# Delta-rule recurrence on one core: next step's products before this step's caps

## What is computed

```
def _cap(S):
    n = jnp.sqrt(jnp.sum(S * S, axis=(-2, -1), keepdims=True))
    return S / jnp.maximum(1.0, n / float(DK))

def step(carry, x):
    S_f, S_s = carry
    qt, kt, vt, bt, fdt, sdt, fgt, sgt = x
    S_f = fdt * S_f
    S_s = sdt * S_s
    err_f = vt - k_t . S_f
    err_s = vt - k_t . S_s
    S_f = S_f + b_t k_t err_f
    S_s = S_s + b_t k_t err_s
    S_fc = _cap(S_f + rf * S_s)
    S_sc = _cap(S_s + rf * S_f)
    ot = fg_t * q_t . S_fc + sg_t * q_t . S_sc
    return ((S_fc, S_sc), ot)
```

## Time and profile before

| | |
|---|---|
| median of 3 runs | 2056.59 us (2056.02 to 2059.79) |
| the profiled execution | 2057.07 us, its span 2055.3 us (1.8 us lie around the span) |
| busy: PE / DVE / ACT / POOL | 77% / 59% / 34% / 4% of the span |
| recurrence, on DVE | from 901.8 to 1186.5 us of the span |
| DVE busy in 992.0 to 1186.5 us | 188.1 of 194.5 us |
| square roots on ACT | 32, 0.21 us each |
| experts, from about 1400 us | PE busy 615 of 655 us |

### The profile page before, as it was taken

The page is one execution under the profiler, slowest core; times in us unless marked ns, Lnnn a source line. Parts: engine busy times, 40 slices in busy tenths (PEclk is TensorE's granted clock), DMA queues, the critical chain, the costliest instruction groups (busy, mean ns, idle before and its releaser), DMA issues. The chain is left out here.

```text
span 2055.3 us, 21772 instructions
## 1 busy us (share of the span) xinstructions
PE 1583.9 (77%) x7119; PEld 1126.0 (55%) x7119; DVE 1208.4 (59%) x2516; ACT 706.4 (34%) x1358; POOL 90.2 (4%) x262
## 2 busy tenths in 40 slices
PE   6999999999599999029200049637999999999993
PEld 3777777777477777003100036335666666666662
DVE  3355555554413988999999933315555555555553
ACT  1333333333145455100000021205555555555550
POOL 0000000000000000002111110030000000000003
PEclk9999999999699999559655559958999999999997
DMA  3101101100215523440000042025454415235004
GB/s 109 33 32 31 31 16 31 31 31 0 86 41 86 87 64 49 61 151 8 0 0 0 0 148 62 1 88 192 176 188 167 170 63 189 91 120 190 21 11 128
DMA packets 116488, 153.31 MB, mean 75 GB/s; under 512 B 47121, under 2 KB 68113, under 8 KB 116401
## 3 DMA queue, kind: packets, MB, share of 16 engines
q1 hardware_dynamic: 110528, 137.81, 22.9%
q0 software_dynamic: 2560, 8.39, 1.2%
q10 hardware_dynamic: 3312, 6.03, 0.8%
HBM read 250.58 MB, written 31.39 MB: 137 GB/s over the span
## 5 line engine op out<-in xcount | busy, mean ns | idle before, releaser
L1482 DVE TENSOR_TENSOR gl<-w_gu,gh 128x2048 fp32r<-128x2048 f32 x138 | 290.8, 2107 | 34.3 <-ACT gh L1429 34.3
L1429 ACT CAST gh<-w_gu 128x2048 fp32r<-128x2048 f32 x138 | 242.2, 1755 | 63.8 <-DMA w_gu<-in_up_proj 53.9
L1394 PE MATMUL bank<-w_d,hT 128*128 128x512 f32 x506 | 242.0, 597 | 8.6 <-ACT hT L1453 8.6
L1371 PE MATMUL bank<-gh,xh 128*128 128x512 f32 (+1 forms) x552 | 219.7, 398 | 11.8 <-DVE xl L1473 11.6
L1496 DVE TENSOR_TENSOR hid<-silu,bank 128x256 f32<-128x256 f32 x138 | 55.1, 399 | 262.7 <-ACT silu L1442 262.6
L1373 PE MATMUL bank<-gh,xl 128*128 128x512 f32 (+1 forms) x552 | 207.6, 376 | 0.0
L1372 PE MATMUL bank<-gl,xh 128*128 128x512 f32 (+1 forms) x552 | 206.6, 374 | 0.0
L1047 PE MATMUL bank<-o_v,o_outw 128*128 128x64 f32 x256 | 36.3, 311 | 215.8 <-DMA o_v<-scratch_v_rows 215.8
L1047 PEld LDWEIGHTS bank<-o_v,o_outw 128*128 128x128 f32 x256 | 36.2, 227 | 219.6 <-DMA o_v<-scratch_v_rows 216.8
L1394 PEld LDWEIGHTS bank<-w_d,hT 128*128 128x128 f32 x506 | 91.8, 188 | 81.3 <-issue 55.2
L927 PE MATMUL bank<-wg,xnT 128*128 128x512 f32 x128 | 61.9, 628 | 88.0 <-DMA bg_row<-in_bg 87.4
(11 more groups left out here) (255 smaller groups left out, 3022.8 us busy)
## 6 DMA issues: line engine op xcount, KB each, us to landing
w_gu<-in_gate_proj SPq DMA_DIRECT2D x46, 1024.0 KB
w_gu<-in_up_proj SPq DMA_DIRECT2D x46, 1024.0 KB
w_d<-in_down_proj SPq DMA_DIRECT2D x46, 1024.0 KB
w_gu<-in_gate_proj SPq DMA_DIRECT2D x23, 768.0 KB
w_gu<-in_up_proj SPq DMA_DIRECT2D x23, 768.0 KB
w_d<-in_down_proj SPq DMA_DIRECT2D x23, 768.0 KB
ctx_raw<-in_ctxT SPq DMA_DIRECT2D x32, 385.5 KB, 3.9
scratch_gram<-gram SPq DMA_DIRECT2D x8, 768.0 KB, 3.3
```

Of the source, the lines that this page charges most:

```text
L1371: pe.matmul(bank, xh[s % 2][:, k, :], hi, start=(k == 0), stop=False)
L1394: mm = pe.matmul(bank, hT[n % 2][:, c, :], w_d[:, b * (BLK // P) + c, :], start=(b == 0 and c == 0), stop=(b == NB - 1 and c == cs[-1]))
L1429: nc.scalar.copy(gh[n % RING][:, :, :, 0:bw].rearrange("p k a f -> p (k a) f"), w_gu[:, :, :, b * BLK:b * BLK + bw].rearrange("p k a f -> ...
L1482: nc.vector.tensor_tensor(gl[n % RING][:, :, :, 0:bw].rearrange("p k a f -> p (k a) f"), w_gu[:, :, :, b * BLK:b * BLK + bw].rearrange("p ...
```

## The change

`link` is no longer used here. `mark(ins)` counts an instruction's end on the semaphore, and `need(n)` makes the next instruction wait for an earlier mark, not for the last one. With these the stream of DVE is written anew:

- `pr` of step t + 1 is made from `psi` of step t + 1 (mixed, but not yet scaled by the cap of that step), right after the mixing and before that step's norm. `pr` has two buffers.
- The products and sums of step t + 1 (`prod`, `vp`) are formed from that `pr` while the norm and the caps of step t are worked out, one instruction of the one between two of the other. Since the cap scales `pr` by one number per state, sums and dots are scaled afterwards: `sc` holds cd and the four products of its pairs, and z[0:2] = vp x cd, z[2:6] = zr x pairs, z[6:9] = n2 x pairs.
- `psi` of step t + 1 is mixed at the end of step t.
- POOL, ACT, PE and SP have the same instructions in the same order.

```diff
--- before.py
+++ after.py
@@ -71,6 +71,16 @@
 
     def __init__(self, eng, sem):
         self.eng, self.sem, self.n, self.base = eng, sem, 0, 0
+
+    def mark(self, ins):
+        self.n += 1
+        ins.then_inc(self.sem, 1)
+        return self.n
+
+    def need(self, n):
+        self.eng.wait_ge(self.sem, self.base + n)
 
     def link(self, ins):
         self.n += 1
...
@@ -862,12 +874,12 @@
         blank = outw[:, 0, 0:C // N, :].rearrange("p j t -> p (j t)")
         prod = sb("r_prod", [P, PROD])
         z, zz, n2 = sb("r_z", [P, NZ, SG]), sb("r_zz", [P, SG, 3, NZ]), sb("r_n2", [P, 3, SG])
-        pr, vp = sb("r_pr", [P, 2, SG, N]), sb("r_vp", [P, 2, SG, N])
+        pr, vp = [sb(f"r_pr{i}", [P, 2, SG, N]) for i in range(2)], sb("r_vp", [P, 2, SG, N])
+        zr, sc = sb("r_zr", [P, 4, SG]), sb("r_sc", [P, 6, SG])
         dots = sb("r_dots", [P, 2, 2, SG, N])
         psi = [sb(f"r_psi{i}", [P, 2, SG, N]) for i in range(PSI)]
         cap = [sb(f"r_cap{i}", [P, 2, SG]) for i in range(PSI)]
         nm, root = sb("r_nm", [P, 2, SG]), sb("r_root", [P, 2, SG])
-        cd, cdd = sb("r_cd", [P, 2, SG]), sb("r_cdd", [P, 3, SG])
         cg, outs, outsum = sb("r_cg", [P, 2, SG]), sb("r_outs", [P, 2, SG, N]), sb("r_outsum", [P, SG, N])
...
@@ -944,52 +956,106 @@
 
             @block.vector
             def _(dve):
-                link = Chain(dve, own).link
+                ch = Chain(dve, own)
+                mark, need = ch.mark, ch.need
                 tt, ts, red = nc.vector.tensor_tensor, nc.vector.tensor_scalar, nc.vector.tensor_reduce
                 stt = nc.vector.scalar_tensor_tensor
                 rf1 = rf[:, 0:1]
                 dve.wait_ge(zeroed, 2)
+
+                def spread_states(t):
+                    u, m = t % PSI, t + 1
+                    if t >= PSI:
+                        dve.wait_ge(out_done, (t - PSI + 1) * POOL_STEPS)
+                    stt(psi[u][:, 0, :, 0:m], phi[:, 1, :, 0:m], rf1, phi[:, 0, :, 0:m], ALU.mult, ALU.add)
+                    return mark(stt(psi[u][:, 1, :, 0:m], phi[:, 0, :, 0:m], rf1, phi[:, 1, :, 0:m], ALU.mult, ALU.add))
+
+                def weights(t):
+                    return mark(tt(pr[t % 2][:, :, :, 0:t], psi[(t - 1) % PSI][:, :, :, 0:t], bc(G[:, None, :, 0:t, 0, t], [2, SG, t]), ALU.mult))
+
+                need(spread_states(0))
+                pr_ready = weights(1)
+                z_ready = dots_ready = None
                 for t in range(N):
-                    u, m = t % PSI, t + 1
-                    if t:
-                        link(tt(pr[:, :, :, 0:t], phi[:, :, :, 0:t], bc(G[:, None, :, 0:t, 0, t], [2, SG, t]), ALU.mult))
-                        rows = [(x, min(x + W, m), min(x + W, t)) for x in range(0, m, W)]
-                        parts, at = [], 0
+                    u, m, nxt = t % PSI, t + 1, t + 1
+                    rows, parts, at = [], [], 0
+                    if nxt < N:
+                        need(pr_ready)
+                        rows = [(x, min(x + W, nxt + 1), min(x + W, nxt)) for x in range(0, nxt + 1, W)]
                         for lo, hi, cols in rows:
                             size = 2 * SG * (hi - lo) * cols
                             parts.append(prod[:, at:at + size].rearrange("p (a s i j) -> p a s i j", a=2, s=SG, i=hi - lo))
                             at += size
-                        for (lo, hi, cols), part in zip(rows, parts):
-                            for a in range(2):
-                                ins = tt(part[:, a], G[:, :, lo:hi, 2, 0:cols],
-                                         bc(pr[:, a, :, None, 0:cols], [SG, hi - lo, cols]), ALU.mult)
-                        link(ins)
-                        for (lo, hi, cols), part in zip(rows, parts):
-                            ins = red(vp[:, :, :, lo:hi].rearrange("p a s i -> p (a s) i"),
-                                      part.rearrange("p a s i j -> p (a s) i j"), AX.X, ALU.add)
-                        link(ins)
-                        nc.vector.tensor_copy(z[:, 0:2, :], vp[:, :, :, t])
-                        for a in range(2):
-                            ins = tt(dots[:, a, :, :, 0:t], vp[:, :, :, 0:t], bc(pr[:, a, None, :, 0:t], [2, SG, t]), ALU.mult)
-                        link(ins)
-                        link(red(z[:, 2:6, :], dots[:, :, :, :, 0:t].rearrange("p a b s t -> p (a b) s t"), AX.X, ALU.add))
-                    link(tt(zz[:, :, :, :], wz[:, :, t, :, :], bc(z[:, :, :].rearrange("p k s -> p s k")[:, :, None, :], [SG, 3, NZ]), ALU.mult))
-                    link(red(n2[:, :, :].rearrange("p r s -> p s r"), zz[:, :, :, :], AX.X, ALU.add))
-                    if t >= PSI:
-                        dve.wait_ge(out_done, (t - PSI + 1) * POOL_STEPS)
+
+                    def products(x, a):
+                        if x < len(rows):
+                            lo, hi, cols = rows[x]
+                            ins = tt(parts[x][:, a], G[:, :, lo:hi, 2, 0:cols], bc(pr[nxt % 2][:, a, :, None, 0:cols], [SG, hi - lo, cols]), ALU.mult)
+                            return mark(ins)
+
+                    def sums(x):
+                        if x < len(rows):
+                            lo, hi, cols = rows[x]
+                            need(made[x])
+                            return mark(red(vp[:, :, :, lo:hi].rearrange("p a s i -> p (a s) i"),
+                                            parts[x].rearrange("p a s i j -> p (a s) i j"), AX.X, ALU.add))
+                        return summed
+
+                    made = [None] * 4
+                    if dots_ready is not None:
+                        need(dots_ready)
+                        raw = mark(red(zr[:, :, :], dots[:, :, :, :, 0:t].rearrange("p a b s t -> p (a b) s t"), AX.X, ALU.add))
+                        products(0, 0)
+                        need(raw)
+                        z_ready = mark(tt(z[:, 2:6, :], zr[:, :, :], sc[:, 2:6, :], ALU.mult))
+                    else:
+                        products(0, 0)
+                    made[0] = products(0, 1)
+                    if z_ready is not None:
+                        need(z_ready)
+                    terms = mark(tt(zz[:, :, :, :], wz[:, :, t, :, :],
+                                    bc(z[:, :, :].rearrange("p k s -> p s k")[:, :, None, :], [SG, 3, NZ]), ALU.mult))
+                    products(1, 0)
+                    need(terms)
+                    norms = mark(red(n2[:, :, :].rearrange("p r s -> p s r"), zz[:, :, :, :], AX.X, ALU.add))
+                    made[1] = products(1, 1)
+                    need(norms)
                     ts(nm[:, :, :], n2[:, 0:3:2, :], 0.0, None, ALU.max).then_inc(nm_ready, 1)
-                    stt(psi[u][:, 0, :, 0:m], phi[:, 1, :, 0:m], rf1, phi[:, 0, :, 0:m], ALU.mult, ALU.add)
-                    stt(psi[u][:, 1, :, 0:m], phi[:, 0, :, 0:m], rf1, phi[:, 1, :, 0:m], ALU.mult, ALU.add)
+                    products(2, 0)
+                    made[2] = products(2, 1)
+                    products(3, 0)
+                    made[3] = products(3, 1)
+                    summed = None
+                    summed = sums(0)
                     dve.wait_ge(root_ready, t + 1)
-                    link(ts(root[:, :, :], root[:, :, :], 1.0, None, ALU.max))
+                    root_kept = mark(ts(root[:, :, :], root[:, :, :], 1.0, None, ALU.max))
+                    summed = sums(1)
+                    need(root_kept)
                     nc.vector.reciprocal(cap[u][:, :, :], root[:, :, :]).then_inc(psi_ready, 1)
+                    if nxt == N:
+                        break
+                    summed = sums(2)
                     dve.wait_ge(psi_ready, t + 1)
-                    if t < N - 1:
-                        link(tt(cd[:, :, :], cap[u][:, :, :], gt[:, :, 1:3, t + 1].rearrange("p s e -> p e s"), ALU.mult))
-                        tt(cdd[:, 0:2, :], cd[:, :, :], bc(cd[:, 0:1, :], [2, SG]), ALU.mult)
-                        link(tt(cdd[:, 2:3, :], cd[:, 1:2, :], cd[:, 1:2, :], ALU.mult))
-                        tt(z[:, 6:9, :], n2[:, :, :], cdd[:, :, :], ALU.mult)
-                        link(tt(phi[:, :, :, 0:m], psi[u][:, :, :, 0:m], bc(cd[:, :, :, None], [2, SG, m]), ALU.mult))
+                    cd_ready = mark(tt(sc[:, 0:2, :], cap[u][:, :, :], gt[:, :, 1:3, nxt].rearrange("p s e -> p e s"), ALU.mult))
+                    summed = sums(3)
+                    need(cd_ready)
+                    phi_ready = mark(tt(phi[:, :, :, 0:m], psi[u][:, :, :, 0:m], bc(sc[:, 0:2, :, None], [2, SG, m]), ALU.mult))
+                    pairs = mark(tt(sc[:, 2:6, :].rearrange("p (a b) s -> p a b s", a=2), bc(sc[:, 0:2, None, :], [2, 2, SG]),
+                                    bc(sc[:, None, 0:2, :], [2, 2, SG]), ALU.mult))
+                    need(summed)
+                    for a in range(2):
```

(10 more changed lines are left out.)

## The result

| | before | after |
|---|---|---|
| median of the runs, us | 2058.19 (2056.02 to 2059.8, 4 runs) | 2025.27 (2022.78 to 2028.24, 4 runs) |
| profiled execution / its span, us | 2057.07 / 2055.3 | 2025.16 / 2023.4 |
| recurrence: root of step 0 to the last reciprocal | 905.67 to 1186.31: 280.6 | 905.67 to 1152.92: 247.2 |
| gaps on DVE in that block (count, us) | 375, 12.8 | 96, 3.8 |

The ratio is 0.9845, with a 95% interval of 0.9827 to 0.9864. Forecast were 2027 us and -29.6; measured are -32.9 by the medians, and -33.4 in the block alone: all of the gain comes from there. (The two profiled executions differ by 31.9; what lies behind the block took 869.0 us in the one and 870.5 in the other, and 869.0 to 874.5 over all the kernels here.) The lengths and the counts of gaps are worked out from the trace (a gap is time in which no DVE instruction runs).

What follows compares the result with a forecast made beforehand. The prediction took the length of DVE's own instruction stream in the recurrence as the bound. Its terms, -31.9 + 2.7 + 0.6 - 1.0 = -29.6 us, gave 2027 us by the median, range 2021 to 2036 us.

Steps and rivals of the forecast that it cites:

- waits removed: DVE's chain in the recurrence: 277 of 372 waits on the instruction just ahead go, at 0.115 us each, -31.9 us.
- one small instruction more per step: DVE, each of 31 steps: one more small instruction at 0.09 us, +2.7 us.
- root no longer covered: ACT's root, once covered by two `psi`: extra waiting in three early steps and at the last, +0.6 us.
- POOL in the way: DVE's two-input instructions stretched by POOL's work in the recurrence: 5.2 us in place of 6.2, -1.0 us.
- The early covers: Waits with an instruction between cost nothing if it takes up at least 0.115 us; products of 256 and more do.
- 1 (2069 us): DVE's waits on its own semaphore drain anyway, so laying work between helps nothing: +12 us, chance 0.03.
- 2 (2063 us): On DVE only the count of instructions decides, and nothing is saved: +6.2 us, chance 0.01.
- 3: POOL takes back part by catching DVE's two-input instructions behind cd: 2041 us at the far end, chance 0.10.
- 4: The change doesn't do what it says, so no change at all: chance 0.01.

Runs made afterwards that it cites:

- e4: Changed kernel with the wait on `pr` moved behind the reduction of dots, to the first product: 2022.14 us.
- e1: Changed kernel, same order of instructions, but every DVE wait on its own semaphore set to the instruction just ahead: 2063.38 us.
- e2: Changed kernel with the next step's products and sums bunched between nm and root, none laid into the chain: 2053.22 us.
- p1: Kernel before the change with POOL's `outs`, `outsum` and `outw` cut to the first token: 2050.93 us.
- p2: Changed kernel with POOL's `outs`, `outsum` and `outw` cut to the first token: 2018.87 us.
- e6: Against e4 with the dots moved between the last links: POOL also starts each step's outputs later, under the sums; 2013.44 us.

## Why the prediction was right, point by point

| term | forecast, us | measured, us |
|---|---|---|
| waits removed | 277 x 0.115 = -31.9 | 279 x 0.122 = -34.0 |
| one small instruction more per step | +2.7 | 31 x 0.093 = +2.9 |
| root no longer covered | +0.6 | +0.4 (0.7 against 0.3) |
| POOL in the way | -1.0 | -0.6 (7.13 to 6.57) |
| step 1 begun ahead of the block | nothing | -0.3 |
| sum | -29.6 | -31.6; the block has -33.4, and 1.8 are not settled |

**The mechanism and the count** came as predicted: 95 waits forecast, 96 gaps seen (92 at such waits and 4 at waits for ACT's root; 372 waits and 375 gaps before), the last reciprocal at 1152.9 where I had said about 1157, and no wait of DVE on POOL's `out_done` at step 8. A wait that is met while another instruction runs costs nothing, which I had from one row; now 15 of the 16 waits of a late step for DVE's own instructions are met so.

**The term that was mis-sized is the first, "0.115 us for each wait on the instruction just ahead".** It was a little low. Measured at the waits themselves the price is 0.114 us in `e4`, 0.118 in `e1` and 0.126 in `e2`. For before against after the nearest measure is `p1` against `p2`, with POOL small in both. Seven kinds of instruction stand in both (root, reciprocal, n2, zz, reduction of dots, dots, phi) and lose 180 gaps and 22.0 us there, 0.122 each. The small ones lose more: the root stood 0.203 us from its successor and now stands 0.071. I had subtracted from the 0.20 us of a linked instruction the 0.09 between the two `cdd`, rows good to a hundredth. Seven thousandths, 279 times, are 2.0 us of the 3.8 that the whole sum was short.

**A term was missing**, put at nothing without a reason. In the changed kernel `pr`, the products and the sum of step 1 come before the root of step 0, while a memset of POOL holds up DVE in both kernels:

```profile
901.86 3.51 POOL L914 MEMSET r_outw<- 128x4096 f32 x1
902.21 0.17 DVE L976 TENSOR_TENSOR r_pr<-r_psi,r_gram 128x8 f32<-128x8 f32 x1
...
903.38 2.02 DVE L1002 TENSOR_REDUCE r_vp<-r_prod 128x16 f32<-128x16 f32 x1
```

The sum of 16 numbers takes 2.02 us and ends 0.03 behind the memset. Before has these instructions in the block, from 906.89 to 907.58. The root of step 0 starts at 905.67 in both, so these 0.7 us are gone; three waits, counted above, are 0.4 of them. 1.8 us are left open; between `p1` and `p2` such a rest lies in hundredths at the products, the sums and the two psi. No two large errors cancelled here: the waits, the missing term and the open rest all err the same way.

**POOL** was sized at 6.2 before and 5.2 after, and is 7.1 and 6.6. Three pieces were off. I left `pr` its 0.70 us at step 30, but POOL's `outsum` was in it, and it takes 0.57 with POOL elsewhere; with POOL small `pr` takes 1.1 us less over the block. I gave the steps up to 23 about 3 us, and by after against `p2` they are 5.6: there pairs, dots, phi and psi, close behind the cap, meet POOL more than that. From step 24 on cd was to meet it for 2 us, and does for 1.0: in four of these eight steps it takes 0.26 to 0.36 us from its start to the next, and in the last four 0.08; at step 30 it starts between `outsum` and `outw`. (The 2.1 us of the fourth sum are 2.2 by the proportion given there; nothing hangs on it.)

**The early covers** were said to hold from 256 numbers on, and below that I counted on products as short as they come. A small one covers only what it is long for. Step 1 of after:

```profile
907.37 0.18 DVE L1009 TENSOR_REDUCE r_zr<-r_dots 128x16 f32<-128x16 f32 x1
907.47 0.18 DVE L995 TENSOR_TENSOR r_prod<-r_gram,r_pr 128x24 f32<-128x24 f32 x1
907.59 0.18 DVE L1012 TENSOR_TENSOR r_z<-r_zr,r_sc 128x16 f32<-128x16 f32 x1
```

The product of 24 numbers covers z's wait but for 0.02 us: z starts 0.12 behind it, not the 0.10 that lie between the two products of 24 in before. No gap shows, since the product's own tail fills it; a few hundredths in a few steps, and the sum did not need them.

**Rivals.** 1 (2069 us) and 2 (2063 us): `e1`, which issues the same instructions with each wait on the one ahead, is 38 us slower than after by the medians, so neither the drain nor the count sets the time. The Trainium skill, "VectorE: DVE Perf Modes", sections "The DRAIN you can't avoid" and "Rules for kernel authors", says that a semaphore behind each instruction costs nothing extra and that the number of instructions is what to reduce. The trace disagrees for dependent instructions: 0.11 to 0.13 us for each wait on the one ahead, and 0.093 for a whole small instruction that waits for nobody. 3: it took back nothing on balance, but `e2` shows that it is real. By the Trainium skill, "SBUF — State Buffer", section "SBUF: two separate sides", an instruction of POOL and one of DVE with two inputs in SBUF exclude each other whole; `p1` and `p2` agree (7.1 and 6.6 us of the block), and one-input sums beside POOL kept their length. 4: the gaps went where they were counted, so no.

## What to carry to other kernels

On an engine that runs a chain of short dependent instructions, count the waits on the instruction just ahead: here each cost 0.11 to 0.13 us, more than one small instruction (0.093), and an independent instruction put between removes that if it is long enough. (An instruction added only for this would gain hundredths by these numbers, which no run here tested.) Price instructions by the distance of their starts, not by their durations. Put what can't be held up (here one-input reductions) beside the other engine's work, and what can be elsewhere; a later start of that engine may be worth as much as a change of one's own.

## What had not been expected of the hardware

- The price of a wait is nearly the same for instructions of 8 and of 120 numbers: by the mean distances of starts, before against after where the link is now free, zz (120 numbers) to its successor went from 0.404 to 0.284 us, n2 from 0.314 to 0.188, the reciprocal (8 numbers) from 0.237 to 0.109.
- POOL is held up by DVE as DVE by POOL: in `e6` `cg` takes 0.90 us (0.21 alone), though each of DVE's instructions there is short. They follow each other without a pause, and `cg` ends at 934.50, when the last one with two inputs (to 934.43) is over:

```profile
933.59 0.41 DVE L999 TENSOR_TENSOR r_prod<-r_gram,r_pr 128x256 f32<-128x256 f32 x1
933.60 0.90 POOL L925 TENSOR_TENSOR r_cg<-r_cap,r_gates 128x8 f32<-128x8 f32 x1
933.93 0.36 DVE L1025 TENSOR_TENSOR r_zz<-r_wz,r_z 128x120 f32<-128x120 f32 x1
934.21 0.22 DVE L999 TENSOR_TENSOR r_prod<-r_gram,r_pr 128x72 f32<-128x72 f32 x1
```

- Durations in the records grow along a stretch without a gap: in `e6` at step 30 the small ones are shown with 0.22 us, as below, and behind cd, which POOL held up, with 0.16 again. Their starts stay 0.07 to 0.09 us apart, so it costs no time; but durations from such a stretch must not be summed or compared. Why is open.

```profile
1126.30 0.22 DVE L1018 TENSOR_TENSOR r_z<-r_zr,r_sc 128x16 f32<-128x16 f32 x1
1126.38 0.47 DVE L999 TENSOR_TENSOR r_prod<-r_gram,r_pr 128x256 f32<-128x256 f32 x1
```
